# A vision-transformer block on one core: layer norm 1 from PSUM, positions as a two-part product, half of the embedding in rounded parts

## The reference, cut to what matters

```python
# x: 32 images of 3 x 64 x 64, cut in 16 x 16 patches: 512 tokens of 768 features; E = 256, 16 heads of 16
h = einsum('bnf,of->bno', patches, W) + b + pos_emb            # 16 tokens an image
z = layernorm(h)
k, q, v = split(z @ W_kqv + b_kqv)
attn = softmax(q k^T / 4 + slopes * tril(j - i), causal)       # per image and head
h = h + (attn v) @ W_proj + b_proj
z = layernorm(h)
r = relu(z @ Wt_fc + 0.05 * (z @ v.T @ fast_b.T @ u.T))        # Wt: ternary rounding of the weights times a row scale
h = h + (r * r) @ Wt_mlp
```

## Time and profile before

| | us |
|---|---|
| median of 3 runs | 68.41 (68.33 to 68.67) |
| the profiled execution, its own time | 68.16 |
| its span (first to last instruction) | 66.4 |
| PE busy | 58.6 (88%) |
| PEld busy | 53.1 (80%) |
| DVE busy | 45.3 (68%) |
| ACT busy | 38.6 (58%) |
| POOL busy | 25.9 (39%) |

### The profile page before, as it was taken

One profiled execution on the slowest core, in us unless ns is written; L12 is line 12 of the kernel. 1 busy time (PEld: TensorE's weight loads), 2 busy tenths in 40 slices (PEclk: granted clock), 3 DMA queues, 4 the chain that ended last, 5 costly groups with the idle time before them and its releaser, 6 DMA issues.

```text
span 66.4 us, 2165 instructions
## 1 busy us (share of the span) xinstructions
PE 58.6 (88%) x894; PEld 53.1 (80%) x894; DVE 45.3 (68%) x97; ACT 38.6 (58%) x78; POOL 25.9 (39%) x43
## 2 busy tenths in 40 slices
PE   5989999999989999999947958999988999999900
PEld 5968588889968999698936846999978999999800
DVE  0000039467999896999799993725999589989660
ACT  5300012824294969974899699830988599783000
POOL 6500007597779569999957100000000000000840
PEclk9999999999999999999999999999999999999996
DMA  0899999999810000000000000000000000000044
GB/s 0 238 352 340 320 392 400 344 387 400 320 42 0 10 0 0 0 10 0 10 0 0 10 5 5 0 10 0 0 0 0 0 0 0 0 0 0 10 161 156
DMA packets 3371, 6.50 MB, mean 98 GB/s; under 512 B 385, under 2 KB 1314, under 8 KB 3362
## 3 DMA queue, kind: packets, MB, share of 16 engines
q1 hardware_dynamic: 3218, 6.24, 26.4%
q10 hardware_dynamic: 144, 0.13, 0.6%
HBM read 5.85 MB, written 0.52 MB: 96 GB/s over the span
## 4 chain that ended last, share of the span: by engine, by line
PE 60%; DVE 18%; ACT 10%; DMA 5%; issue 3%
PE psum L307 12%; PE psum L467 12%; PE psum L493 11%; PE psum L373 5%; PE psum L347 5%; DMA head_sb<-head 5%; PE psum L313 3%; PE psum L402 3%; DVE z L787 3%; PE psum L476 2%; PE psum L327 2%; DVE prob_n L850 2%; DVE bn L779 2%; DVE prob_t L857 2%; ACT zt_hi L610 2%
## 5 line engine op out<-in xcount | busy, mean ns | idle before, releaser
L1051 POOL TENSOR_TENSOR tail_sb<-tail_sb,h 128x256 f32<-128x256 f32 x3 | 2.1, 734 | 25.0 <-DVE tail_sb L886 25.0
L493 PE MATMUL psum<-mlp_t,sq_lo 128*128 128x256 f32 x32 | 7.7, 281 | 0.0
L493 PE MATMUL psum<-mlp_t,sq_hi 128*128 128x256 f32 x32 | 7.7, 280 | 0.0
L601 ACT ACTIVATE std<-mv,eps_sb 128x1 f32<-128x1 f32 x8 | 2.4, 294 | 8.8 <-DVE mv L781 8.8
L777 DVE TENSOR_TENSOR h<-psum,posb 128x256 f32<-128x256 f32 x4 | 1.6, 412 | 8.5 <-PE psum L307 8.5
L467 PE MATMUL psum<-zt_hi,fc_t 128*128 128x256 f32 x32 | 6.9, 287 | 0.5 <-ACT zt_hi L610 0.5
L726 ACT ACTIVATE head_sb<-psum,fc_scale 128x256 f32<-128x256 f32 x16 | 6.7, 471 | 0.7 <-DVE kqv_sb L897 0.7
L467 PE MATMUL psum<-zt_lo,fc_t 128*128 128x256 f32 x32 | 6.7, 279 | 0.0
L493 PEld LDWEIGHTS psum<-mlp_t,sq_lo 128*128 128x128 f32 x32 | 6.0, 189 | 0.0
L493 PEld LDWEIGHTS psum<-mlp_t,sq_hi 128*128 128x128 f32 x32 | 6.0, 189 | 0.0
L307 PE MATMUL psum<-head_sb 128*128 128x256 f32 x24 | 5.7, 389 | 0.3 <-DMA head_sb<-head 0.3
(11 more groups left out here) (112 smaller groups left out, 158.8 us busy)
## 6 DMA issues: line engine op xcount, KB each, us to landing
head_sb<-head SPq DMA_DIRECT2D x6, 256.0 KB, 3.7
fc_sb<-w_fc SPq DMA_DIRECT2D x2, 512.0 KB, 6.9
mlp_sb<-w_mlp SPq DMA_DIRECT2D x2, 512.0 KB, 8.7
tail_sb<-tail SPq DMA_DIRECT2D x2, 384.0 KB, 5.9
out<-tail_sb SPq DMA_DIRECT2D x3, 128.0 KB, 1.7
kqv_sb<-w_k SPq DMA_DIRECT2D x1, 256.0 KB, 6.3
kqv_sb<-w_q SPq DMA_DIRECT2D x1, 256.0 KB, 6.5
kqv_sb<-w_v SPq DMA_DIRECT2D x1, 256.0 KB, 5.8
```

The costliest lines, as they stand in the source:

```text
L493: mm = pe.matmul(mlp_ps[f * BH + b], part[:, n % RING, a, b * P:(b + 1) * P], mlp_t[:, 2 * j + a, :], start=j == 0 and a == 0 and i == 0 a ...
L601: nc.scalar.activation(std[:, which, b:b + 1], mv[:, which, b, 1:2], ACT.Sqrt, bias=eps_sb[:, 0:1]).then_inc(std_ready, 1)
```

## The change

1. **Positions.** The host gives the position rows twice, in rows 0 to 16 and 32 to 48 of a load that now has 49 rows (rows 17 to 31 are zero). ACT rounds all of them to fp32r (`pos_r`), DVE replaces the lower copy of the values by what rounding left, and one product per block (`embed_pos`) adds both parts in the block's own bank. The product, copy and bank of before (`pos_ps`, `posb`) are gone.
2. **Layer norm 1.** DVE takes statistics and normalises straight from PSUM; its add is gone. ACT copies each block from PSUM to `h1` later (`hidden_copy`). PE waits for three of the copies before `value(0)` and for all before `key(1)`, which write the banks.
3. **Blocks 2 and 3 in rounded parts.** ACT makes high parts of the six weight pieces (`embed_weight_high`) and of the tail's tokens (`tail_high`), DVE the low ones of the weights and of block 3's tokens, POOL those of block 2's. Block 2 keeps two full products (k = 0, 1), its other four and all six of block 3 become three products each. The parts lie in buffers that are used later in the program (`sq_hi`, `sq_lo`, `fc_t`, `mlp_t`), by whose names they show.
4. **Order.** Blocks 0 and 1 alternate in k = 4 and 5. ACT does `ident_bf` and `select_r`, which POOL did. POOL makes V's low part ahead of the bias parts. DVE takes block 3's normalising ahead of `key_copy(0)`, and block 2's statistics ahead of `zt_low(0)`. `residual(1)` goes behind `value_factors`.

```diff
@@ sync, tensor
-        pos_sb = sb("pos_sb", [S + 1, P + E])
+        pos_sb = sb("pos_sb", [POS_ROWS, P + E])      # POS_ROWS = 32 + 16 + 1
...
+            def embed_pos(b, stop=False):
+                return pe.matmul(tok_ps[b], pos_r[:, 0:P], pos_r[:, P:P + E], start=False, stop=stop)
...
+            def embed_tail_high(b):
+                pe.wait_ge(tail_hi_ready, b - BH + 1)
+                pe.wait_ge(split_lo, KF)
+                for k in range(SPLIT[b - BH], KF):
+                    embed_tail(k, b, tail_hi, emb_hi)
+                    embed_tail(k, b, tail_hi, emb_lo)
+
+            def embed_tail_low(b):
+                pe.wait_ge(tail_lo_ready, b - BH + 1)
+                for k in range(SPLIT[b - BH], KF):
+                    mm = embed_tail(k, b, tail_lo, emb_hi, stop=k == KF - 1)
+                mm.then_inc(tok_done, 1)
...
+            pe.wait_ge(h1_ready, 3)
             value(0)
...
             pe.wait_ge(k_copied, 1)
+            pe.wait_ge(h1_ready, BLOCKS)
             key(1)
@@ scalar
-            copy_out(posb[:, :], pos_ps, pos_done, 1, posb_ready)
+            for k in range(LAST):
+                embed_weight_high(k)
+            act.wait_ge(pos_in, 16)
+            nc.scalar.activation(pos_r[:, :], pos_sb[:, :], ACT.Copy).then_inc(pos_step, 1)
+            for k in range(LAST, KF):
+                embed_weight_high(k)
+            tail_high(0)
             norm_std(0, 0, var1, std1)
             norm_std(1, 0, var1, std1)
+            tail_high(1)
+            act.wait_ge(const_in, 16)
+            nc.scalar.activation(ident_bf[:, :], ident, ACT.Copy).then_inc(ident_half, 1)
             weight_high(K, k_in, k_w_hi)
             weight_high(Q, q_in, q_w_hi)
             copy_out(zt_hi[0][:, :, :], zt_ps[0][:, :], zt_turned, 1, zt_hi_ready)
             norm_std(2, 0, var1, std1)
             weight_high(V, v_in, v_w_hi)
+            nc.scalar.activation(select_r[:, :, :], select.rearrange(...), ACT.Copy).then_inc(select_done, 1)
+            hidden_copy(0)
+            hidden_copy(1)
             norm_std(3, 0, var1, std1)
+            hidden_copy(2)
+            hidden_copy(3)
@@ vector
-                dve.tensor_tensor(hidden_state[:, b, :], src, other, ALU.add).then_inc(h_sem, 1)
-                dve.wait_ge(h_sem, b + 1)
-                dve.bn_stats(bn6[:, which, b, :], hidden_state[:, b, :]).then_inc(bn_sem, 1)
+                dve.bn_stats(bn6[:, which, b, :], hidden_state).then_inc(bn_sem, 1)
@@ gpsimd
+            pool.wait_ge(tail_hi_ready, 1)
+            pool.tensor_tensor(tail_lo[0][:, SPLIT[0]:, :], tail_sb[:, 0, SPLIT[0]:, :], tail_hi[0][:, SPLIT[0]:, :].bitcast(F32),
+                               ALU.subtract).then_inc(tail_lo_ready, 1)
             bias_tables()
             weight_low(K, k_w_hi, k_w_lo)
             weight_low(Q, q_w_hi, q_w_lo)
+            weight_low(V, v_w_hi, v_w_lo)
             bias_parts()
-            weight_low(V, v_w_hi, v_w_lo)
...
             residual(0)
-            residual(1)
...
             value_factors()
+            residual(1)
```

More of the change, by code:

```diff
@@ L41 @@
 FOLD = 4 * 2 * RANK
+POS_LOW = 32
+POS_ROWS = POS_LOW + S + 1
 C_ID = 0
@@ L154, in build_program @@
         sq_lo = sb("sq_lo", [P, RING, 2, HT], F32R)
+        SPLIT = (2, 0)
+        emb_hi, emb_lo = (t[:, :, :, :].rearrange("p r a t -> p (r a t)")[:, 0:KF * E].rearrange(
+            "p (k n) -> p k n", n=E) for t in (sq_hi, sq_lo))
+        tail_hi, tail_lo = ([t[:, :, :].rearrange("p m n -> p (m n)")[:, i * FEAT:(i + 1) * FEAT].rearrange(
+            "p (k t) -> p k t", t=P) for t in (fc_t, mlp_t)] for i in range(2))
         out_sb = tail_sb[:, :, :, :].rearrange("p b k t -> p (b k t)")[:, 0:BLOCKS * E].rearrange(
@@ L190, in build_program @@
         q_zero = sem("q_zero")
-        pos_done, posb_ready = sem("pos_done"), sem("posb_ready")
+        pos_step = sem("pos_step")
         select_done = sem("select_done")
@@ L507, in _ @@
                     embed(k, b)
[L508 to L514, removed]
-            pe.wait_ge(tail_in[0], 16)
-            for k in range(KF):
-                mm = embed(k, 2)
-            mm.then_inc(tok_done, 1)
+            for k in range(LAST, KF):
+                pe.wait_ge(head_in[k], 16)
+                for b in range(BH):
+                    embed(k, b)
+                    if k == KF - 1:
+                        pe.wait_ge(pos_step, 2)
+                        embed_pos(b, stop=True).then_inc(tok_done, 1)
+            pe.wait_ge(tail_in[0], 16)
+            for k in range(SPLIT[0]):
+                embed(k, 2)
+            embed_pos(2)
+            embed_tail_high(2)
+            embed_tail_low(2)
             pe.wait_ge(const_in, 16)
             turn(0, z, zt_ps[0], z1_ready, zt_turned)
[L521 to L524, removed]
+            embed_tail_high(3)
+            embed_pos(3)
+            embed_tail_low(3)
             key(0)
@@ L684, in _ @@
             weight_high(V, v_in, v_w_hi)
+            nc.scalar.activation(select_r[:, :, :], select.rearrange("p (o s) -> p o s", o=1).broadcast_to(
+                [P, HPG, S]), ACT.Copy).then_inc(select_done, 1)
+            hidden_copy(0)
+            hidden_copy(1)
             norm_std(3, 0, var1, std1)
+            hidden_copy(2)
+            hidden_copy(3)
             key_spread(0, (0,))
@@ L904, in square_low, with embed_weight_low @@
                          sq_hi_ready, sq_lo_ready)
-            dve.wait_ge(posb_ready, 1)
+            def embed_weight_low(k):
+                low_part(emb_lo[:, k, :], head_sb[:, k, HT:HT + E], emb_hi[:, k, :], k + 1,
+                         split_hi, split_lo)
+            for k in range(LAST):
+                embed_weight_low(k)
+            low_rows = slice(POS_LOW, POS_ROWS)
+            low_part(pos_r[low_rows, P:P + E], pos_sb[low_rows, P:P + E], pos_r[low_rows, P:P + E], 1, pos_step, pos_step)
+            for k in range(LAST, KF):
+                embed_weight_low(k)
             stats1(0)
@@ L1101 @@
     consts[:, C_VB:C_END] = b_v.T
+    positions = np.zeros((POS_ROWS, P + E), np.float32)
+    for row in (0, POS_LOW):
+        positions[row:row + S, 0:P] = np.tile(np.eye(S, dtype=np.float32), (1, IPB))
+        positions[row + S, 0:P] = 1.0
+        positions[row:row + S, P:] = a(L0_tok_pos_emb)
+        positions[row + S, P:] = a(L0_tok_b)
     arrays = {
         "head": np.concatenate([x_t[:, :, 0:HT], by_partition(a(L0_tok_W).T)], axis=2),
-        "pos": np.concatenate([np.concatenate([np.tile(np.eye(S, dtype=np.float32), (1, IPB)), np.ones((1, P), np.float32)]),
-                               np.concatenate([a(L0_tok_pos_emb), a(L0_tok_b).reshape(1, E)])], axis=1),
+        "pos": positions,
         "tail": x_t[:, :, HT:TOK].reshape(P, KF, BH, P).transpose(0, 2, 1, 3),
```

50 lines of the change are left out of this document (33 added, 17 removed).

## The result

The change makes the kernel slower. Its median is 70.18 us (69.92 to 70.61, 4 runs) against 68.54 of the kernel before on the same chip, a ratio of 1.0256 with the interval 1.0179 to 1.0333; on a second chip it was 69.79 (69.74 to 70.06, 4 runs) against 68.77, 1.0175 (1.0083 to 1.0268). The forecast was 66.8, with a range of 66.3 to 67.8. The profiled execution took 70.34 us, 68.6 of them its span.

A forecast was written before the change was run, and what follows sets the result against it. TensorE was taken as the bound from 7.5 us until the scores. Four terms (-0.60, -0.19, -0.35, -0.49) sum to -1.63: 68.16 to 66.5 us in the profiled run, 66.8 as median, range 66.3 to 67.8.

The forecast's parts named there:

- term 1: Positions on PE: two cheap position products replace the full-precision one, block 2 starts at 9.34 instead of 9.94: -0.60 us.
- Term 1's other half: Load of head[4]: 49 position rows dealt to seven DMA engines, so it lands 0.6 us earlier, near 7.2.
- rival C: Position load: all 49 packets on one DMA engine, PE idle before k = 4, +0.8 us to 69.3; chance 0.08.
- rival B: Position load doesn't make head[4] earlier; k = 4 starts near 7.9, 0.5 us back, 67.3; chance 0.35 with Rival A.
- Terms 2 and 3: Embedding of blocks 2 and 3 on PE: rounded products take 2.40 and 2.24 for 2.59 each: -0.19 and -0.35 us.
- Term 4: turn(1) on PE: four transposes take 0.44 instead of 0.93 without the wait for block 3's z: -0.49 us.
- The covers: Added work on ACT, DVE and POOL finishes before PE wants it, with 0.1 to 0.5 us to spare at the thinnest places.
- Rival A: Splitting engines ACT or POOL end last; PE waits at key(0) or scores, costing 0.3 to 1.0 us; chance 0.35 with rival B.
- Rival D: No shift: PE's gain is lost later, as an engine behind the scores has its own bound; 68.4, chance 0.04.

The follow-up runs named there:

- pos128: The change with the position rows zero-padded from 49 to 128 for the position product, the load staying at 49 rows: 68.38 us, 0.9953 of the kernel before.
- before_warm36: The kernel before with 36 warm-up products (12 of 128 columns, 24 of 64) instead of 24, total columns unchanged: 1.012 of the kernel before.
- pos128_warm20: pos128 with 20 warm-up products instead of 24, so 902 TensorE products instead of 906, profiled once: 68.82 us.
- full_tail: The change without its part 3: blocks 2 and 3 embedded in full precision, splits left out: 69.58 us, 1.0123 of the kernel before.
- before_z3_first: The kernel before with block 3 normalised ahead of the key copy on DVE, nothing else changed: 1.0012 of the kernel before.
- pos128_warm12: pos128 with 12 warm-up products of 256 columns instead of 24 of 128: 67.76 us, 0.9777 of the kernel before.
- best_again: pos128_warm12 unchanged, run once more in more runs: 67.48 us, 0.9821 of the kernel before.
- best_fill: pos128_warm12 with 6 warm-up products of 512 columns and 7 idle products between fold_v and project(0): 67.41 us, 0.9782 of the kernel before.
- after_warm12: The change with 12 warm-up products of 256 columns instead of 24 of 128: 0.9981 of the kernel before.

## Why the prediction was wrong

By its own steps, in the execution of the change with the full clock:

| | forecast | measured | difference |
|---|---|---|---|
| k = 4 begins (term 1) | 7.37 | 7.84 | +0.47 |
| first tail product | 9.34 | 10.52 | +1.18, of it 0.71 new |
| `key(0)` | 14.42 | 16.48 | +2.06, of it 0.88 new |
| scores | 19.58 | 21.57 | +1.99 |
| from there to the end of the span | 45.2 | 46.3 | +1.1 |

- **The step that failed is the price of the position product** in terms 1 to 3: 0.118 was that of a rounded product on 128 rows, and these have 49. It costs 0.51 in its place, 1.57 us for the four, which is nearly all of the 1.63 that the forecast gained until the scores. The earlier trace rows had it: the 17-row product held the weight loads from 7.46 to 8.09, 0.63 us for two records of 0.216, and the weight loads stand still for 0.33 ahead of each of the two rows. The profile named loads as what ended both; I took them as waits that would go, and never asked whether they would come back four times. pos128 shows both the cause and the price.
- **Not forecast at all: the stop in `values(1)`**, 1.36 us, 1.1 to 1.2 of them at the end. I counted the 12 additional products by their columns alone, and took all that follows the scores to keep its length. It is the number of instructions that moved the border; before_warm36 shows it without any of the change, pos128_warm20 its place.
- **Term 1's other half** (`head[4]`): the load was dealt out to seven engines as worked out, and rival C did not come. But `head[4]` landed 0.1 to 0.4 earlier, not 0.6 (7.73 in this trace), and PE had its first 16 records done at 7.84, not 7.37: of all profiles, that of before was the earliest there. So rival B's price of 0.5 was paid, for its own reason and for a second one at the same place: I had read the times of the loads and of the clock from one execution.
- **Terms 2 and 3, the rounded parts**, were right once the row count is taken out: 2.40 and 2.32 in pos128 for 2.40 and 2.24; full_tail shows 0.20 and 0.29 of gain for 0.19 and 0.35.
- **Term 4** was right: 0.35 for the turn of half 1 where 0.44 was put, and 0.58 gained for 0.49. That it was worth something only together with the other edits, as its neighbour POOL is next, is shown by before_z3_first.
- **The covers** held. Rival A did not come: PE never waits for a split part. Normalising from PSUM costs 0.12 more each, just outside of the 0.1 allowed, and nothing waits for it.
- Rival D (no shift) was wrong as put: pos128_warm12, which has neither the row change nor the stop, took 67.05 and 67.39 us in its two executions at the full clock, near the forecast. best_again's ratio of 0.9821 is a gain of 1.2 us, about the 1.63 less the 0.5 of rival B.

In sum: 64.8 us of span forecast (66.4 - 1.63), + 0.5 (k = 4) + 1.57 (row count) + 1.1 (stop) = 67.97; measured 67.9. The first profile is 0.7 longer: its clock rose at 6.2 us, not at 4.3, and its scores began at 22.23.

What stays open: why the clock rose anywhere from 3.5 to 7.3 us, though PE's first product starts at 0.77 in every trace; what decides when the packet of an instruction block begins; and what PE still waits for once it is over.

## What to carry to other kernels

Give every product in a dense stretch of TensorE the same number of rows: pad the operand with zeros if need be, since an odd one (49 rows here, 17 in before) cost 0.39 us beyond its columns. Count TensorE's instructions, not only their columns: where a long row of tiny products met a border of the instruction stream it stood for up to 1.63 us, and 12 instruction pairs less ahead of it, made wider in their place, moved the border behind a wait. Look at the new trace for where the border went: best_fill has it in the scores, best_again a short one in `values(0)`. And where a short product lies between others in the trace of before, take its whole length, start to start of its neighbours, as the price of the next one like it.

## What the runs showed of the hardware that I had not expected

- A product on 49 or 17 rows between 128-row ones costs time on both sides. Among full-precision neighbours the records start at 7.15, 7.46, 7.78, 8.09 and 8.41 in before (17 rows, two records; 0.216 apart elsewhere); among rounded ones at 15.15, 15.36, 15.67 and 15.89 in block 3 of the change (0.118 apart elsewhere): 0.39 above the columns there too.
- PE stood for 1.05 to 1.63 us at a fixed place of its instruction stream (and for 0.23 to 1.51 at two earlier ones), and went on 2.3 to 2.9 us after a 16 KB packet of its instruction queue began.
- The clock's rise to 2.4 GHz came between 3.5 and 7.3 us after the first instruction in the 14 profiles; until then a full-precision record takes 0.43 instead of 0.216 us. Two profiles of the same kernel differ by it: the first tail product came at 11.18 and 10.52 in the change (rise at 6.2 and 4.3), at 10.46 and 10.01 in pos128_warm12 (6.4 and 5.5).
- A low clock in the middle needn't cost time of its own: in the first profile `values(1)` began 1.5 us after the packet and had no stop, probably as the missing block was there by the time it was wanted, and the time from the scores to the end was the 46.3 us of the execution at full clock. pos128, which has the stop, took 68.04 to 68.53 us in four executions with a mean clock of 0.965 to 0.974, no longer than its full-clock ones (68.1 to 68.82), though a fifth (0.975) took 69.52; after_warm12, whose trace has no stop, took 69.86 to 70.32 in its five executions with a low clock and 68.61 to 68.83 in four of the other five.
